# Experts' second layer in three fp32r parts for three of four chunks, with one high part cast by GpSimd

## The reference, cut to what matters

```python
x = x + L0_attn(layernorm(x))          # 16 heads, weights 1/(eps + distance)^2
# L0_ffn: 8 experts of hidden size 512, the two best per token are mixed
h = relu(einsum('bsd,edh->ebsh', input_emb, W1) + b1[:, None, None, :])
expert_out = einsum('ebsh,ehd->ebsd', h, W2) + b2[:, None, None, :]
x = x + einsum('bse,ebsd->bsd', routed, expert_out)
x = x + L1_attn(layernorm(x))          # linear attention, 16 heads of 8
x = x + L1_ffn(layernorm(x))           # the top 384 of 512 tokens become gelu(x @ w_block)
```

## Time and profile before

| | us |
|---|---|
| median of 3 runs | 1422.97 |
| lowest, highest | 1420.4, 1423.03 |
| the profiled execution, its own time | 1423.09 |
| its span, first to last instruction | 1421.3 |
| PE busy (share of the span) | 1388.2 (98%) |
| ACT busy | 1100.7 (77%) |
| DVE busy | 1091.0 (77%) |
| POOL busy | 840.3 (59%) |

### The profile page before, as it was taken

How to read it: one execution, slowest core, us unless ns; L and a number is a source line. 1 busy time by engine, 2 the same in 40 slices (tenths; PEclk the granted TensorE clock), 3 DMA queues, 4 the chain that set the end, 5 groups by cost and what they waited for, 6 DMA issues and landing times.

```text
span 1421.3 us, 18230 instructions
## 1 busy us (share of the span) xinstructions
PE 1388.2 (98%) x6486; PEld 743.3 (52%) x6486; DVE 1091.0 (77%) x2046; ACT 1100.7 (77%) x951; POOL 840.3 (59%) x657
## 2 busy tenths in 40 slices
PE   8999999999999999999999999899999999999996
PEld 5444444444443444444444444445777777777675
DVE  7887887888888887887888778635677686776857
ACT  2799889979978979979979979944676776776752
POOL 4568777778778778868877876411333433333330
PEclk9999999999999999999999999999999999999999
DMA  3000110101101101101101012442011010110100
GB/s 113 1 17 17 24 46 17 23 25 38 24 17 46 24 17 33 37 17 31 39 16 32 16 30 61 115 142 106 1 68 60 8 68 1 68 60 8 68 1 15
DMA packets 45705, 54.99 MB, mean 39 GB/s; under 512 B 13808, under 2 KB 32368, under 8 KB 44464
## 3 DMA queue, kind: packets, MB, share of 16 engines
q1 hardware_dynamic: 45616, 53.84, 12.6%
HBM read 48.97 MB, written 4.85 MB: 38 GB/s over the span
## 4 chain that ended last, share of the span: by engine, by line
PE 86%; DVE 8%; ACT 5%; issue 1%; DMA 0%; DVEq 0%; SPq 0%; ACTq 0%
PE sc L406 14%; PE av L419 13%; PE z L74 12%; PE pj L74 12%; PE y L1221 8%; PE sc L401 6%; PE y L74 5%; PE pj L383 4%; PE pj L451 4%; DVE w L597 3%; PE pj L429 2%; ACT w L684 1%; ACT w L688 1%; ACT w L680 1%; DVE high L565 1%
## 5 line engine op out<-in xcount | busy, mean ns | idle before, releaser
L597 DVE TENSOR_SCALAR w<-sc 128x1024 f32<-128x1024 f32 x256 | 301.2, 1217 | 70.0 <-PE sc L406 68.9
L680 ACT ACTIVATE w<-w 128x2048 f32<-128x2048 f32 x128 | 237.5, 1904 | 123.6 <-DVE w L597 123.2
L320 POOL TENSOR_TENSOR wsum<-wsum,w 128x512 f32<-128x512 f32 x248 | 317.9, 1282 | 19.4
L969 POOL TENSOR_TENSOR hr_l<-hr,hr_h 128x512 fp32r<-128x512 f32 x112 | 151.9, 1356 | 263.1 <-ACT hr L1025 263.1
L406 PE MATMUL sc<-query,key 64*128 64x512 f32 x1024 | 243.1, 594 | 0.0
L684 ACT ACTIVATE w<-w 128x2048 f32<-128x2048 f32 x128 | 240.1, 1899 | 0.4
L688 ACT ACTIVATE w<-w 128x2048 f32<-128x2048 f32 x128 | 239.8, 1897 | 0.0
L419 PE MATMUL av<-w,vt 128*64 128x512 f32 x1024 | 233.8, 598 | 2.6 <-ACT w L688 2.5
L1025 ACT ACTIVATE hr<-z,b 128x512 f32<-128x512 f32 x256 | 173.4, 684 | 67.7 <-PE z L74 67.6
L306 POOL TENSOR_TENSOR sqq<-query 128x512 f32<-128x512 f32 x63 | 65.6, 1042 | 187.6 <-DVE query L537 147.4
L317 POOL TENSOR_TENSOR wsum<-w 128x512 f32<-128x512 f32 x124 | 159.4, 1285 | 5.2 <-ACT w L688 5.2
(11 more groups left out here) (215 smaller groups left out, 2362.5 us busy)
## 6 DMA issues: line engine op xcount, KB each, us to landing
hT<-head_recips SPq DMA_DIRECT2D x64, 256.0 KB, 3.9
rb<-routing SPq DMA_DIRECT2D x8, 2048.0 KB, 6.9
w<-in_W SPq DMA_DIRECT2D x16, 256.0 KB, 4.8
xa<-in_X SPq DMA_DIRECT2D x8, 256.0 KB, 4.5
xc<-in_X SPq DMA_DIRECT2D x8, 256.0 KB, 2.7
x<-xc SPq DMA_DIRECT2D x8, 256.0 KB, 3.9
x<-x SPq DMA_DIRECT2D x1, 1792.0 KB, 7.9
out<-prod SPq DMA_DIRECT2D x7, 256.0 KB, 2.3
```

The source lines that it names most:

```text
L320: nc.gpsimd.tensor_tensor(wsum[:, u, :], wsum[:, u, :], w[:, j % 2, u, c, :], ALU.add).then_inc(s_added, 1)
L597: nc.vector.tensor_scalar(w[:, s, 2 * r:2 * r + 2, c, :], sc[:, i, :, :], 0.0, None, ALU.max).then_inc(s_d2, 1)
L680: nc.scalar.activation(w[:, j % 2, u, :, :], w[:, j % 2, u, :, :], ACT.Sqrt).then_inc(s_sqrt, 1)
```

## The change

- `in_parts(n)` becomes n % 4 > 0 from batch 1 on: 24 units of a batch instead of 16. The new units are those with n % 4 = 2.
- In the new units (`by_pool`) ACT writes only `hr`. POOL casts it to the high part, waits for that on a semaphore of its own (`hi`), and subtracts. In the others ACT writes the high part as before.
- The parts of `w2` hold three of four chunks. The low ones lie where `w1` was; DVE's scratch for the ranks is no longer in `w1` but has two rows of its own, so DVE waits after each of the four rank steps (N_T 11 to 14, N_R 4 to 7). `split_w2` runs in units 25 to 32, and PE waits for it expert by expert.
- Places (without those of LATE): on DVE `add_experts` and the first sums from 9 to 8, `kept` and results from 7 to 9, `tail_norm` from 11 to 12, `softmax_end`, `expert_ranks` and `routing` each one later; on ACT `root_t` from 11 to 12, `turned_t` from 16 to 17, `exponential` from 23 to 24, `turned_routing` from 30 to unit 0 of the next batch; on PE `turn_t` from 10 to 11, `turn_routing` from 24 to 26.

```diff
-            return n >= NU and n % 2 == 1
+            return n >= NU and n % NF > 0
+
+        def by_pool(n):
+            return in_parts(n) and n % NF == 2
+
+        def part(n):
+            return n // NF * (NF - 1) + n % NF - 1
...
-            for n in range(NU + 1, B * NU, 2):
-                m = n // 2
-                pool.wait_ge(S["hr"], n + 1)
-                nc.gpsimd.tensor_tensor(hrs[1][:, m % (HR // 2), :], hr[:, n % HR, :],
-                                        hrs[0][:, m % (HR // 2), :].bitcast(F32), ALU.subtract).then_inc(S["lo"], 1)
+            n_hi = 0
+            for n in range(NU, B * NU):
+                if in_parts(n):
+                    high, low = hrs[0][:, part(n) % HP, :], hrs[1][:, part(n) % HP, :]
+                    pool.wait_ge(S["hr"], n + 1)
+                    if by_pool(n):
+                        n_hi += 1
+                        nc.gpsimd.tensor_copy(high, hr[:, n % HR, :]).then_inc(S["hi"], 1)
+                        pool.wait_ge(S["hi"], n_hi)
+                    nc.gpsimd.tensor_tensor(low, hr[:, n % HR, :], high.bitcast(F32), ALU.subtract).then_inc(S["lo"], 1)
...
-                if in_parts(n):
+                if in_parts(n) and not by_pool(n):
...
-                    if k == at(t, 11):
+                    if k == (11 if t == LATE else 12):
...
                         root_t(t, 0)
-                    if k == at(t, 16):
+                    if k == (15 if t == LATE else 17):
                         turned_t(t, 0)
...
-                    if k == 23:
+                    if k == 24:
                         exponential(f)
-                    if k == 30:
-                        turned_routing(f)
+                if 1 <= b < B and k == 0:
+                    turned_routing(b)
...
-                if n == NU + 1:
-                    pe.wait_ge(S["w2s"], NE * NF)
...
+                    if b == 1 and i == 1:
+                        pe.wait_ge(S["w2s"], 2 * (NF - 1) * (k // NF + 1))
...
-                    if k == at(t, 10):
+                    if k == (9 if t == LATE else 11):
...
                         turn_t(t, 0)
...
-                    if k == 24:
+                    if k == 26:
                         turn_routing(f)
...
-                if c == NC - 1:
+                if t < LATE or c == NC - 1:
                     lr(t, ins)
...
-                    if k == 7:
+                    if k == 9:
                         kept(u)
...
-                    if k == 9:
+                    if k == 8:
...
                         add_experts(t)
                         tail_stats(t, 0)
-                    if k == at(t, 11):
+                    if k == (11 if t == LATE else 12):
                         tail_norm(t, 0)
...
-                    if k == 24:
+                    if k == 25:
                         softmax_end(f)
-                    if k == 25:
+                    if k == 26:
                         expert_ranks(f)
-                    if k == 26:
+                    if k == 27:
                         routing(f)
```

More of the change, by code:

```diff
@@ L772, in psum @@
             return own.enter_context(nc.psum_tensor(name, shape, F32))
-        w1 = sb("w1", [P, NE, FF])
+        with ExitStack() as until_split:
+            w1 = until_split.enter_context(nc.sbuf_tensor("w1", [P, NE, FF], F32))
+        w2_l = sb("w2_l", [P, NE * (NF - 1), D], F32R)
+        scr = sb("scr", [P, 2, T])
         w2 = sb("w2", [P, NE * NF, D])
@@ L859, in build_rest @@
         N_F = 13
-        N_T, N_R = 11, 4
+        N_T, N_R = 14, 7
         LATE = B - 2
@@ L1019, in hidden @@
                 act.wait_ge(S["z"], n + 1)
-                if in_parts(n):
+                if in_parts(n) and not by_pool(n):
                     if n == NU + 1:
                         act.wait_ge(att["x1_out"], 16 * B)
-                    nc.scalar.activation(hrs[0][:, n // 2 % (HR // 2), :], z[:, n % 2, :], ACT.Relu,
+                    nc.scalar.activation(hrs[0][:, part(n) % HP, :], z[:, n % 2, :], ACT.Relu,
                                          bias=b1[:, n % NU:n % NU + 1])
@@ L1212, in expert @@
                     pe.wait_ge(S["rwT"], 1)
-                if n == NU + 1:
-                    pe.wait_ge(S["w2s"], NE * NF)
                 pe.wait_ge(S["hr"], n + 1)
                 if in_parts(n):
-                    pe.wait_ge(S["lo"], (n - NU) // 2 + 1)
-                    m = product(nc, y[:, g % 2, :], [w[:, k // 2, :] for w in w2s],
-                                [v[:, n // 2 % (HR // 2), :] for v in hrs], start=False, stop=(i == NF - 1))
+                    if b == 1 and i == 1:
+                        pe.wait_ge(S["w2s"], 2 * (NF - 1) * (k // NF + 1))
+                    pe.wait_ge(S["lo"], part(n) - part(NU + 1) + 1)
+                    m = product(nc, y[:, g % 2, :], [w[:, part(k), :] for w in w2s],
+                                [v[:, part(n) % HP, :] for v in hrs], start=False, stop=(i == NF - 1))
                 else:
@@ L1487, in split_w2 @@
             def split_w2(e):
[L1488 to L1493, removed]
+                parts = slice((NF - 1) * e, (NF - 1) * (e + 1))
+                source = w2[:, NF * e + 1:NF * (e + 1), :]
+                V.tensor_copy(w2s[0][:, parts, :], source).then_inc(S["w2s"], NF - 1)
+                dve.wait_ge(S["w2s"], (NF - 1) * (2 * e + 1))
+                V.tensor_tensor(w2s[1][:, parts, :], source, w2s[0][:, parts, :].bitcast(F32),
+                                ALU.subtract).then_inc(S["w2s"], NF - 1)
             def weigh(g):
@@ L1590, in step @@
                     add_output(B - 1)
-                if b == 0 and k >= 24:
-                    if k == 24:
+                if 25 <= n < 25 + NE:
+                    if n == 25:
                         dve.wait_ge(att["x1_out"], 16 * B)
-                    dve.wait_ge(in_w2[k - 24], 16)
-                    split_w2(k - 24)
+                    dve.wait_ge(in_w2[n - 25], 16)
+                    split_w2(n - 25)
             att_step, weighted_values, sums, reciprocals, output, add_output = att_vector(dve)
```

19 lines of the change are left out of this document (12 added, 7 removed).

## The result

| | before | after |
|---|---|---|
| median of 8 runs each, us | 1422.3 | 1426.96 |
| lowest, highest | 1420.4, 1423.03 | 1424.31, 1428.01 |
| ratio of the runs, 95% interval | 1 | 1.0032 [1.0023, 1.0041] |
| the profiled execution; its span | 1423.1; 1421.3 | 1428.0; 1426.2 |

The changed kernel is slower by 4.7 us, in the direction of the forecast of 1442.9, but by a quarter of the forecast 19.8 us.

The account below looks back on a forecast made before the run. PE's instruction stream was taken to bound the experts' stage. From 1423.1 us, 9.0 came off for the matmuls and 28.8 were added for DVE held by POOL: 1442.9 us, range 1412 to 1458.

Parts of the forecast that it names:

- Part 1, the matmuls: PE, experts' stage: 56 fp32 matmuls become three fp32r each, saving 0.16 us each, 1.3 per batch, 9.0 in all.
- Part 2, POOL: Experts' stage: subtraction 1.29 us, cast 1.04; POOL works 39 us per batch instead of 22; PE waits for no low part.
- Part 3, the hold: POOL's work holds DVE's chains and PE waits: 4.8 us per batch, six batches, +28.8 us.
- One for one: With POOL instructions queued, the engines alternate; each lockable DVE instruction of a chain waits for a whole POOL instruction.
- Chain A: DVE's results, sums and first norm, batches 2 to 7: PE loses 4.0 us at `xn_t`'s turn; 2.7 taken per batch.
- the walk: Step-by-step timing of both DVE chains under POOL's queue: 4.0 and 3.2 us per batch, two thirds of each taken.
- Chain B: DVE's ranks and second norm, batches 1 to 6: `z` of unit 33 waits 3.2 us; 2.1 taken per batch.
- Part 4: Other edits (rank waits, `split_w2`, later root, exponential, `turned_t`, routing broadcast) cost nothing; if `split_w2` lost its cover, 1.6 us once.
- No stall: Rival, chance 0.34: DVE's chains pass or the new places fit; -9.0 with up to 2 us given back, 1414 to 1416.
- The point from which it decides: Experts' stage: below 1.5 us of stall per batch the changed kernel is faster.

Follow-up runs that it names:

- experiment 2: The changed kernel with POOL's casts and subtractions of `hr` cut to 8 of 512 columns: 1410.66 us, ratio 0.9916 to the kernel before.
- experiment 6: Here, experiment 1 with PE's turn of the scores one unit later (30 instead of 29, batches 0 to 5): 1409.9 us, ratio 0.9917.
- The dose: The changed kernel with POOL's cast at 0.20 us (8 columns) or 1.04 (product of `hr` with itself) instead of 0.61: 1414.47 and 1443.12 us.
- the halves: The changed kernel with each of POOL's subtractions done as two of 256 columns: 1416.19 us, ratio 0.9962 to the kernel before.
- Experiment 1: The changed kernel with `kept` and the eight results back from unit 9 to 7, ahead of the sums: 1413.34 us, ratio 0.9938 to the kernel before.
- the long cast: The changed kernel with POOL's cast replaced by a product of `hr` with itself, 1.04 us: 1443.12 us, ratio 1.0151 to the kernel before.
- the parts alone: The changed kernel with all places put back to those of before: 1429.6 us, ratio 1.0053 to the kernel before.
- The places alone: The kernel before with only the place changes, two of four chunks in parts, no POOL cast: 1417.93 us, ratio 0.9965.
- the short cast: The changed kernel with POOL's cast on 8 of 512 columns, 0.20 us: 1414.47 us, ratio 0.9944 to the kernel before.

## Why the prediction was half right

**Part 1, the matmuls: right.** 56.16 us for a batch without a wait was the forecast's sum, and 56.12 to 56.16 were measured in experiments 2 and 6.

**Part 2, POOL: its load right, the price of the cast wrong.** The subtraction took 1.29 again and POOL 38 us of a batch. PE waits for no low part at any place. But the cast takes 0.61 us, not 1.04. I had bounds of 0.42 and 1.29, and took the middle by the square of one tile, because it was the nearest row. The operand count was the wrong measure of near: the square reads its tile twice. This is the mis-sized term. The dose shows what it is worth: 16.2 us between 0.61 and 1.04, where the forecast was 15.9 too high. That the two agree is in part luck, as the clock below shows.

The 769 ns that the Trainium skill (GPSIMD Engine Reference, "Elementwise — side-by-side cycle accounting") gives for 512 elements was 0.16 too high as well, but closer than my row. I had costed it at 0.5 us per batch, from POOL's work alone; by the dose the batch has about 2 us less at 0.77 than at 1.04, if one interpolates between the two measured lengths.

**Part 3, the hold: mechanism right, sizes off in both directions.** One for one was right: four `xn_t` of 1.12 us stretched to 4.49, ranks of 0.42, 1.53, 0.72 and 1.40. The Trainium skill (SBUF — State Buffer, "Who interferes with whom") has the lock for the whole of an instruction, and with the halves `xn_t` shrinks just as POOL's instruction does: the trace agrees.

*Chain A* was named with its place (the turn of `xn_t`, DVE its releaser) and its cause, the results between sums and norm. Experiment 1 confirms both. It cost 1.8 us per steady batch where 2.7 was taken: the last `xn_t` ended 18.4 us into the batch, and the walk had it at 20.7. With the long cast in the kernel it ended at 19.1, so the walk was 1.6 us too long at its own price too: eight of the chain's instructions were held and not ten, since the second `keep` took 0.16 us beside POOL's cast and the sum of `yT` came behind the norm. In the last batch it cost 3.2 us and 1.65 of clock.

*Chain B* is the step that failed: 2.1 us per batch were taken for a `z` that waits for `hr` behind the second root, and in the changed kernel no steady batch has that wait. The timelines of DVE, ACT and PE, changed kernel, batch 4:

```profile
1200.42 0.42 DVE L1382 TENSOR_TENSOR gt<-pr 128x256 f32<-128x256 f32 x1
1200.75 1.53 DVE L1383 TENSOR_TENSOR eq<-pr 128x256 f32<-128x256 f32 x1
1202.32 0.72 DVE L1384 TENSOR_TENSOR eq<-eq,etri 128x256 f32<-128x256 f32 x1
1203.07 1.40 DVE L1385 TENSOR_TENSOR gt<-gt,eq 128x256 f32<-128x256 f32 x1
...
1208.62 0.28 DVE L734 BATCH_NORM_AGGREGATE mv_t<-stats_t 128x2 f32<-128x6 f32 x3
...
1210.13 2.70 DVE L743 TENSOR_SCALAR xn_t<-x,mv_t,rstd_t 128x128 f32<-128x128 f32 x4
```

```profile
1207.68 0.69 ACT L1048 ACTIVATE hr<-z,b 128x512 f32<-128x512 f32 x1 [0.29 <-PE z L74]
1208.39 1.28 ACT L749 ACT_TABLE_LOAD   x1
1209.68 0.21 ACT L749 ACTIVATE std_t<-mv_t 128x4 f32<-128x4 f32 x1
```

```profile
1211.38 0.39 PE L74 MATMUL z<-xs_h,w_h 128*128 128x512 f32 x1
...
1214.34 0.65 PE L1207 MATMUL tb<-ident,score 128*128 128x128 f32 x4
```

Two of its terms were too dear. The ranks are held for 1.3 us more than before, not 3.1, since a short cast is in the queue and one instruction gets through. And I had put the table load behind ACT's wait for `mv_t`. It began at 1208.39, at once behind `hr`, while the last `mv_t` was still to come (1208.62 to 1208.90): the load does not stand behind the root's wait. So its 1.28 us lie beside DVE's delay, and `z` of unit 33 is on time at 1211.38 with no idle ahead of it. The trace of the kernel before already held such a row, at the exponential of batch 0:

```profile
963.80 1.28 ACT L989 ACT_TABLE_LOAD   x1
968.92 0.23 ACT L989 ACTIVATE pr<-lg 128x32 f32<-128x32 f32 x1 [3.84 <-DVE lg L1347]
```

The load ended at 965.08, and the exponential waited another 3.84 us for its input. Two other causes can be ruled out. That PE was late already by chain A does not explain the missing wait: experiment 1 has no wait of chain A, and no `z` of batches 1 to 7 waits there either. Nor does the cast's price: with the long cast all four ranks are held (1.51, 1.26, 1.39 and 1.40 us in batch 4, 5.55 instead of 2.74 in all, near the walk's 3.1 more), ACT's root waits 0.49 us behind its load, and PE's `z` behind it waits 0.03 us. What is late next in chain B is what I had not walked: the second norm, held to 2.70 us, and PE's turn of the scores, 0.3 to 0.6 us in six batches, which experiment 6 removed. A root that holds `hr`, and a `z` that waits for it, do occur with the parts alone (0.4 us in batches 2 to 6, 3.2 in the last), but at the first root of a batch, behind the results, and not at the second.

By chains, measured against the batches of experiment 2 and with experiment 1 to part them: A cost 14 us in all, its clock fall in it, where 16.2 were taken; B 2.7, at the scores, where 12.6 were taken. So in the kernel as it is most of the stalls' error lies in chain B, and the cast's price does not make it good: with the long cast the wait at the scores is 0.71 us a batch, a third of the 2.1.

**Not foreseen: the clock.** The forecast had no term for it. In the changed kernel it is one fall, 1.65 us, in the last batch. With the long cast it is a fall in nearly every batch, some 10 of the 21 us over the kernel before. The agreement of 1443.12 with 1442.9 is therefore partly two errors that cancel: in that kernel the waits of a steady batch were 3.7 us against my 4.8, and the clock made up the rest.

**Part 4: right that it costs nothing, wrong that it gains nothing.** In batch 0 of the kernel before, ACT's exponential waited 3.8 us for `lg` (the rows under chain B), with `hr` queued behind it. The waits of before, from 940 to 990 us:

```profile
PE z L74 <- ACT hr L1025: 1.4, 1, 1.4
```

The 1.4 is the longest of the earlier trace rows, which I had read and not followed. With the exponential one unit later ACT waits 1.4 us instead of 3.8, PE's wait of 1.4 is gone, and batch 0 is 1.5 us shorter. The places alone gained 4.1 us of batches in all, against 0 in the forecast.

**The rivals.** No stall, 1414 to 1416, is what the change gives once the results stand at 7 (1413.3), so it missed by one place. The point from which it decides, 1.5 us of stall per batch, was right: 2.2 us made the kernel slower.

## What to carry to other kernels

Where POOL and DVE share work, count for a DVE chain that PE waits for how many POOL instructions can be queued while it runs: here each held DVE instruction of the chain ended with one whole POOL instruction, so keep such a chain short, put independent DVE work ahead of it and not into it, and cut POOL's instructions in pieces before you cut POOL's work. Measure the price of an operation that the trace does not show before choosing among places: here 0.84 us in one POOL instruction, eight times a batch, lay between a gain of 0.6% and a loss of 1.5%. Look in the trace for how ACT's table load stands to the wait of its instruction before you walk a chain through it. A new wait of one microsecond ahead of TensorE may cost more than that microsecond; look at the granted clock behind it.

## What the runs showed of the hardware

- While POOL had instructions queued, DVE's `tensor_scalar` of 128x128 in fp32 (0.34 us alone) alternated with them one for one: four took 1.35, 0.63, 1.45 and 1.30 us beside POOL's 1.28, 0.61, 1.28 and 1.26. With each subtraction in two halves of 0.74 the longest was 0.88.
- A POOL cast of 128x512 from fp32 to fp32r takes 0.61 us, against 1.04 for a product that reads one tile twice and 1.29 for a subtraction of two tiles; on 8 columns it takes 0.20, and a subtraction of 256 columns 0.74.
- ACT's table load was not held by the wait of the instruction it is loaded for: it began at 1208.39, 0.5 us ahead of the end of that instruction's input, and in batch 0 of the kernel before it was over 3.84 us ahead of the exponential.
- TensorE's clock fell from 2.4 to 1.2 GHz behind waits of 1.02 and 0.90 us (long cast, each of batches 2 to 6), behind 1.23, 0.22 and 1.02 (last batch of the changed kernel), and behind 1.23 and 0.89 (last batch with the short cast). It did not behind 0.57 and 0.89, nor behind 0.68, 0.35, 0.22 and 0.48 (last batch with the halves). Two of these falls were priced, at 1.65 and 1.7 us in the matmuls behind them. What exactly sets it was not tried.
- The start of the experts' stage differs by up to 2.9 us between profiled executions of kernels that are the same up to there; its cause stays open.
